# Gated feed-forward with two experts on one Trainium2 core: the rarer expert's weights as a difference to the common one's, formed on GpSimd

## The reference

```
vm = expert_mask(token_type_ids)[..., None]
x = rms_norm(hidden_states, ln_in_w)
mixed = jnp.where(vm, x @ v_qkv, x @ l_qkv)          # q, k, v
...
attn_out = jnp.where(vm, ctx @ v_dense, ctx @ l_dense)
...
mi = rms_norm(hidden_states, ln_post_attn_w)
v_out = jax.nn.silu(mi @ v_gate) * (mi @ v_up) @ v_down
l_out = jax.nn.silu(mi @ l_gate) * (mi @ l_up) @ l_down
hidden_states = hidden_states + jnp.where(vm, v_out, l_out)
```

## Time and profile before

| | us |
|---|---|
| median of 3 runs | 2722.21 |
| lowest, highest | 2719.45, 2730.94 |
| the profiled execution | 2724.13 |
| its span, first to last instruction | 2722.3 |
| mean granted TensorE clock | 0.994 of 2.4 GHz |

### The profile page before, as it was taken

One profiled execution on the slowest core, in us unless ns is written; L12 is line 12 of the kernel. 1 busy time (PEld: TensorE's weight loads), 2 busy tenths in 40 slices (PEclk: granted clock), 3 DMA queues, 4 the chain that ended last, 5 costly groups with the idle time before them and its releaser, 6 DMA issues.

```text
span 2722.3 us, 52680 instructions
## 1 busy us (share of the span) xinstructions
PE 2627.3 (97%) x19429; PEld 1584.6 (58%) x19429; DVE 1624.8 (60%) x3532; ACT 1318.6 (48%) x4818; POOL 974.3 (36%) x862
## 2 busy tenths in 40 slices
PE   6999999999999999999999999999999999999998
PEld 4556566665555656566556565656655556566664
DVE  2426567786424547777643454777855345477874
ACT  2446444654343644464444373555534447255452
POOL 0014344553111515555311241654621133155452
PEclk9999999999999999999999999999999999999999
DMA  7000021212201011120220101112121010120111
GB/s 204 1 24 13 21 55 36 52 29 71 67 1 36 2 31 51 30 64 22 70 63 1 35 2 47 43 30 55 29 71 55 1 36 2 51 58 19 48 29 55
DMA packets 171044, 109.52 MB, mean 40 GB/s; under 512 B 31714, under 2 KB 168356, under 8 KB 170660
## 3 DMA queue, kind: packets, MB, share of 16 engines
q1 hardware_dynamic: 166336, 105.82, 14.0%
q10 hardware_dynamic: 4452, 0.29, 0.1%
HBM read 101.87 MB, written 4.19 MB: 39 GB/s over the span
## 4 chain that ended last, share of the span: by engine, by line
PE 81%; DVE 10%; ACT 5%; issue 2%; POOL 1%; ACTq 1%; DVEq 0%
PE bank L1334 11%; PE bank L1351 6%; PE bank L979 5%; PE bank L1057 5%; PE bank L1239 4%; PE bank L1227 4%; PE bank L1248 4%; PE bank L1220 4%; PE bank L1274 3%; ACT Ebuf L1438 3%; PE bank L1340 3%; PE bank L1033 2%; PE bank L1074 2%; PE bank L1211 2%; PE bank L1017 2%
## 5 line engine op out<-in xcount | busy, mean ns | idle before, releaser
L1839 POOL TENSOR_TENSOR Ebuf<-Ebuf,row_rcp 128x512 f32<-128x512 f32 (+1 forms) x328 | 344.4, 1056 | 956.6 <-DVE row_rcp L1655 956.4
L1438 ACT ACTIVATE Ebuf<-bank,minus_max 128x64 f32<-128x64 f32 x1568 | 468.3, 333 | 116.3 <-DVE minus_max L1639 115.4
L1639 DVE TENSOR_REDUCE minus_max<-bank 128x8 f32<-128x512 f32 (+1 forms) x328 | 220.3, 674 | 226.2 <-PE bank L1017 124.5
L1438 ACT ACTIVATION_READ_ACCUMULATOR Ebuf<-bank,minus_max 128x1 f32 x1568 | 353.5, 225 | 0.0
L1447 ACT ACTIVATE PT<-bank 128x512 f32<-128x512 f32 (+1 forms) x328 | 193.7, 603 | 128.2 <-PE bank L1057 125.8
L1057 PE MATMUL bank<-ident,Ebuf 128*128 128x128 f32 x1296 | 200.9, 281 | 10.0 <-POOL Ebuf L1839 9.5
L1057 PEld LDWEIGHTS bank<-ident,Ebuf 128*128 128x128 f32 x1296 | 146.8, 142 | 79.2 <-issue 46.2
L1334 PE MATMUL bank<-xs_b,w_ring 128*128 128x512 f32 (+1 forms) x384 | 170.0, 605 | 2.4 <-DVE xs_b L1733 2.4
L1334 PE MATMUL bank<-xs_a,w_ring 128*128 128x512 f32 (+1 forms) x384 | 168.8, 602 | 0.0
L966 PE MATMUL bank<-causal_bf,ident_bf 128*128 128x512 bf16 x525 | 136.8, 383 | 0.0
L1881 POOL TENSOR_TENSOR arena_b<-arena_b,masks_b 128x384 f32<-128x384 f32 (+1 forms) x48 | 67.7, 1411 | 192.7 <-DVE arena_b L1809 192.6
(11 more groups left out here) (322 smaller groups left out, 5668.8 us busy)
## 6 DMA issues: line engine op xcount, KB each, us to landing
w_ring<-in_L_W SPq DMA_DIRECT2D x64, 256.0 KB, 3.1
w_ring<-in_L_l_gate SPq DMA_DIRECT2D x80, 128.0 KB, 2.2
w_ring<-in_L_l_up SPq DMA_DIRECT2D x80, 128.0 KB, 2.3
w_ring<-in_L_l_down SPq DMA_DIRECT2D x80, 128.0 KB, 2.2
w_ring<-in_L_v_gate SPq DMA_DIRECT2D x80, 128.0 KB, 2.4
w_ring<-in_L_v_up SPq DMA_DIRECT2D x80, 128.0 KB, 2.4
w_ring<-in_L_v_down SPq DMA_DIRECT2D x80, 128.0 KB, 2.5
arena_a<-in_x SPq DMA_DIRECT2D x4, 512.0 KB
```

The source lines that it names most:

```text
L1438: last = A(Ebuf[:, u % UNITS, cell], bank(token)[:, cell], ACT.Exp, bias=minus_max[:, u % UNITS, c:c + 1], accum_out=row_sum[:, u % UNITS, ...
L1639: V.reduce_max(minus_max[:, u % UNITS, 0:g], cells(bank(token)[:, 0:g * S]), AX_X, negate=True).then_inc(maxed, 1)
L1839: G_.tensor_tensor(v, v, row_rcp[:, n % 3, 0:g].unsqueeze(2).broadcast_to([P, g, S]), ALU.mult).then_inc(probs_ready, 1)
```

## The change

The common expert's products now take every token, unmasked, and the rarer expert's weights are replaced by their difference to the common ones, v - l; x l + (mask x)(v - l) is the same sum. The gate's part is masked, so that the hidden units of the rarer part are silu(g) masked, times u.

- Lines 1726, 1729 and 1814 are gone; `spread` writes xn directly, and lines 1733 and 1853 read xn and write xv. xn_ready is counted once more per half. is_l becomes a constant 1 (`all`) that the attention's line 1757 still reads.
- `u` on VectorE: one product into hid_l, then, after GpSimd's product, one over the late columns: hid_v times u (from PSUM) times 0.5. u's PSUM bank is free after the latter.
- New on GpSimd: `weigh`, three subtractions in the ring for each chunk, after its loads and before TensorE's `g`; a part of `silu`, the late columns of silu_g times is_v into hid_v; once, behind the first `zero_s`, the subtractions of the resident q, k, v and dense weights. The early mask (line 1881) now reads hid_l.
- The plan: new costs (weigh 1.7, silu's GpSimd part 0.45, u on VectorE 1.0 for 2.4, spread 1.75 for 3.45 and 1.15 for 2.0), weigh with its own nominal time, slots given out in the plan's order of weigh and l1h, and both of these held until the slot's last reader has ended and 10 us (`LOADED`) have passed. All engines' lists and the fillers are made anew from this.

```diff
@@ -137,7 +137,7 @@
     for j in range(FT):
-        steps += [(6.4 * j, "g", n, j), (6.4 * j + 1.5, "silu", n, j), (6.4 * j + 2.1, "u", n, j), (6.4 * j + 10.6, "down", n, j)]
+        steps += [(max(0.0, 6.4 * j - 9.0), "weigh", n, j), (6.4 * j, "g", n, j), (6.4 * j + 1.5, "silu", n, j), (6.4 * j + 2.1, "u", n, j), (6.4 * j + 10.6, "down", n, j)]
     return steps + [(6.4 * FT + 6.4, "res3", n)], 6.4 * FT + 6.4
@@ -237,8 +238,10 @@
         return [("POOL", 2.15, None)]
+    if step == "weigh":
+        return [("POOL", 1.7, None)]
     if step == "u":
-        return chain(*(() if where[1] == FT - 1 else (("PE", 2.2),)), ("DVE", 2.4), ("POOL", 1.4))
+        return chain(*(() if where[1] == FT - 1 else (("PE", 2.2),)), ("DVE", 1.0), ("POOL", 1.4))
     if step == "g" and where[1] == FT - 1:
@@ -306,10 +309,12 @@
+    if step == "weigh":
+        return of("PE", ("g", n, last - 1)) if last else of("DVE", ("sums", 5 if n == 2 else 8, 0))
...
-        return of("DVE", ("spread", 5 if n == 2 else 8, 1)) + of(None, ("silu", n, last - 2)) + of("DVE", ("u", n, last - 2))
+        return of(None, ("weigh", *where)) + of("DVE", ("spread", 5 if n == 2 else 8, 1)) + of(None, ("silu", n, last - 2)) + of("DVE", ("u", n, last - 2))
...
-        return of(None, ("silu", *where)) + of("PE", ("down", n, last - 2)) + (of("DVE", ("u", n, last - 1)) if last == FT - 1 else [])
+        return of(None, ("silu", *where)) + of("PE", ("down", n, last - 2)) + of("POOL", ("u", n, last - 2)) + (of("DVE", ("u", n, last - 1)) if last == FT - 1 else [])
@@ -397,10 +403,22 @@
+    def slot():
+        if len(chunks) < SLOTS:
+            return 0.0
+        when = end.get((chunks[len(chunks) - SLOTS][1], "PE"))
+        return None if when is None else when + LOADED
     def room(token):
...
         key = where[0] if where else None
+        if step == "weigh":
+            return slot()
+        if step == "l1h" and where[0] % 2 == 0:
+            there, free = slot(), banks(1)
+            return None if there is None or free is None else max(there, free)
         if step in FILL_STEPS and parts(step, where)[0][0] == "PE":
@@ -796,7 +809,7 @@
-            return {"g": g_ready, "u": h_ready}[step][s].at(turn, FT * li + last + 1)
+            return {"g": g_ready, "u": hv_late}[step][s].at(turn, FT * li + last + 1)
@@ -1317,11 +1330,11 @@
                         rows = P if j < FT - 1 else FR
-                        ring, there = chunk("ffn", s, turn, n, j)
+                        ring, _ = chunk("ffn", s, turn, n, j)
                         w = ffn_weights(ring)[0][step]
...
                         if step == "g":
-                            pe.wait_ge(*there)
+                            pe.wait_ge(*weighed[s].at(turn, FT * (n - 2) + j + 1))
                             if j == 0:
@@ -1345,7 +1358,7 @@
-                        pe.wait_ge(*hl_ready[s].at(turn, FT * (n - 2) + j + 1))
+                        pe.wait_ge(*h_ready[s].at(turn, FT * (n - 2) + j + 1))
@@ -1553,9 +1566,8 @@
                     if j >= 2:
-                        act.wait_ge(*hl_ready[s].at(turn, k - 1))
-                        act.wait_ge(*hv_late[s].at(turn, k - 1))
-                        act.wait_ge(*hv_early[s].at(turn, k - 1))
+                        act.wait_ge(*h_ready[s].at(turn, k - 1))
+                        act.wait_ge(*sv_ready[s].at(turn, k - 1))
                     act.wait_ge(*g_ready[s].at(turn, k + 1))
@@ -1625,7 +1637,7 @@
-                    V.tensor_scalar(st.is_l[:, :], st.is_v[:, :], -1.0, 1.0, ALU.mult, ALU.add).then_inc(masks_ready[s].sem, 1)
+                    V.memset(st.all[:, :], 1.0).then_inc(masks_ready[s].sem, 1)
@@ -1710,8 +1722,8 @@
                     src = st.xn if n in (1, 2) else st.xT
-                    dst, ready = {0: (st.xT, x0_ready), 4: (st.xn, xn_ready), 7: (st.xn, xn_ready), 1: (st.xn, normed),
-                                  2: (st.xn, normed)}.get(n, (st.xv, normed))
+                    dst, ready = {0: (st.xT, x0_ready), 1: (st.xn, normed),
+                                  2: (st.xn, normed)}.get(n, (st.xn, xn_ready))
                     for m in range(DT):
@@ -1720,17 +1732,9 @@
                             V.tensor_scalar(st.xn[:, m, :], st.xn[:, m, :], shift, None, ALU.add).then_inc(xn_ready[s].sem, 1)
-                    if n in (3, 6):
-                        for m in range(DT):
-                            dve.wait_ge(*normed[s].at(turn, STEP_AT[n] + m + 1))
-                            V.tensor_tensor(st.xn[:, m, :], st.xv[:, m, :], st.is_l[:, :], ALU.mult).then_inc(xn_ready[s].sem, 1)
-                    if n in (5, 8):
-                        dve.wait_ge(*normed[s].at(turn, STEP_AT[n] + 2 * h + 2))
-                        V.tensor_tensor(st.xn[:, :, at], st.xv[:, :, at], both(st.is_l[:, at]), ALU.mult).then_inc(xn_ready[s].sem, 1)
                     if n in LATE_AT:
-                        dve.wait_ge(*xn_ready[s].at(turn, XN_AT[n] + (h + 1 if n in HALVED else 2)))
-                        v = late(st.xv[:, :, at])
-                        V.tensor_tensor(v, v, late(both(st.is_v[:, at])), ALU.mult).then_inc(xv_late[s].sem, 1)
+                        dve.wait_ge(*xn_ready[s].at(turn, XN_AT[n] + 2 * h + 2))
+                        V.tensor_tensor(late(st.xv[:, :, at]), late(st.xn[:, :, at]), late(both(st.is_v[:, at])), ALU.mult).then_inc(xv_late[s].sem, 1)
                 if step == "l1v":
@@ -1806,14 +1810,15 @@
                         up = st.g_copy[0:rows, 1 - j % 2, :]
-                    V.scalar_tensor_tensor(out=v, in0=v, scalar=0.5, in1=up,
-                                           op0=ALU.mult, op1=ALU.mult).then_inc(h_ready[s].sem, 1)
-                    dve.wait_ge(*h_ready[s].at(turn, k + 1))
                     if j >= 2:
                         dve.wait_ge(*down_done[s].at(turn, k - 1))
-                    V.tensor_tensor(st.hid_l[0:rows, j % 2, :], v, st.is_l[0:rows, :], ALU.mult).then_inc(hl_ready[s].sem, 1)
-                    V.tensor_tensor(by_batch(st.hid_v[0:rows, j % 2, :])[:, :, LATE:S], by_batch(v)[:, :, LATE:S],
-                                    by_batch(st.is_v[0:rows, :])[:, :, LATE:S], ALU.mult).then_inc(hv_late[s].sem, 1)
+                        dve.wait_ge(*hv_early[s].at(turn, k - 1))
+                    V.scalar_tensor_tensor(out=st.hid_l[0:rows, j % 2, :], in0=v, scalar=0.5, in1=up,
+                                           op0=ALU.mult, op1=ALU.mult).then_inc(h_ready[s].sem, 1)
+                    dve.wait_ge(*sv_ready[s].at(turn, k + 1))
+                    hv = by_batch(st.hid_v[0:rows, j % 2, :])[:, :, LATE:S]
+                    V.scalar_tensor_tensor(out=hv, in0=hv, scalar=0.5, in1=by_batch(up)[:, :, LATE:S],
+                                           op0=ALU.mult, op1=ALU.mult).then_inc(hv_late[s].sem, 1)
                 if step == "res3":
@@ -1844,13 +1849,20 @@
                     G_.memset(st.arena[:, A_VS:A_VS + 2048], 0.0).then_inc(v_zeroed[s].sem, 1)
+                    if turn == 0 and s == 0:
+                        for n in (2, 3):
+                            pool.wait_ge(w_loaded[n], 16 * 9)
+                            for of in (w_qkv, w_dense):
+                                rare, other = of[n, "v"][:, :, :], of[n, "l"][:, :, :]
+                                last = G_.tensor_tensor(rare, rare, other, ALU.subtract)
+                            last.then_inc(w_weighed, 1)
                 if step == "spread" and where[0] in LATE_AT:
...
                     at = span(n, h)
-                    pool.wait_ge(*xn_ready[s].at(turn, XN_AT[n] + (h + 1 if n in HALVED else 2)))
+                    pool.wait_ge(*xn_ready[s].at(turn, XN_AT[n] + 2 * h + 2))
                     for m in range(DT):
-                        v = by_batch(st.xv[:, m, at])[:, :, 0:LATE]
-                        last = G_.tensor_tensor(v, v, by_batch(st.is_v[:, at])[:, :, 0:LATE], ALU.mult)
+                        v, x = (by_batch(some[:, m, at])[:, :, 0:LATE] for some in (st.xv, st.xn))
+                        last = G_.tensor_tensor(v, x, by_batch(st.is_v[:, at])[:, :, 0:LATE], ALU.mult)
                     last.then_inc(xv_early[s].sem, 1)
@@ -1872,13 +1884,31 @@
                         G_.tensor_tensor(*cross_blocks(st, p, r), ALU.mult).then_inc(kbd_built[s].sem, 1)
+                if step == "weigh":
+                    n, j = where
+                    rows = P if j < FT - 1 else FR
+                    ring, there = chunk("ffn", s, turn, n, j)
+                    into, down = ffn_weights(ring)
+                    pool.wait_ge(*there)
+                    for of in "gu":
+                        rare, other = (into[of][e][:, :, 0:rows] for e in "vl")
+                        G_.tensor_tensor(rare, rare, other, ALU.subtract)
+                    G_.tensor_tensor(down["v"][0:rows, :], down["v"][0:rows, :], down["l"][0:rows, :], ALU.subtract).then_inc(weighed[s].sem, 1)
+                if step == "silu":
```

(9 more changed lines are left out.)

43 lines of the change are left out of this document (21 added, 22 removed).

## The result

The changed kernel takes 2742.9 us (median of 20 runs, 2729.0 to 2752.6) against 2720.0 us for the kernel before on the same chips. The ratio of the mean times is 1.0069, 95% interval 1.0054 to 1.0085. It is **slower by 19 us** by the means and by 23 us by the medians, where I forecast 25 us faster. One run of each kernel, at 5210.8 and 7364.7 us, stands far off all others and is in neither the range nor the ratio. The profiled run took 2746.45 us, with a span of 2744.6 and a mean granted clock of 0.990.

The account below looks back on a forecast made before the run. TensorE, busy 97%, was taken as the bound, so only 232 us of its idle time and fillers could give. Direct gain 20, shorter VectorE queue 10, GpSimd loss 5: -25 us, 2697 us against the 2722.2 median; range 2650 to 2750.

Parts of the forecast that it names:

- rival C: Beside attention, weighing on GpSimd delays softmax products and VectorE waits; 30% of 204 us on the path: 2753 us; chance 0.15.
- Steps 1 and 2, 3: VectorE loses 193 us of mask work: 20 us direct gain on the chain, 10 us from its shorter queue.
- Step 4: GpSimd gets 212 us of weighing, late mask and resident subtractions; idle time hides the latter's 8 us at the start.
- Step 5: On GpSimd's fixed queue, 204 us of recurring work delays softmax products: 5 us lost, ends 0 and 102 us.
- Step 6a: TensorE's first matmul on a chunk waits for weighing; at the last chunk 1.3 us fit into 11.5.
- Step 7: GpSimd's new time meets some 850 two-SBUF-input VectorE instructions by chance: 24 us on VectorE, 2 on the path.
- rival D: GpSimd's shared access with VectorE lies on the path: 48 us less the 30 gained, +18, 2740 us; chance 0.07.

Follow-up runs that it names:

- e2: e1 with the streamed weighing left out, GpSimd writing one column per chunk instead; 2690.3 us, ratio 0.9864 to 0.9906.
- e1: Changed kernel with the resident qkv and dense subtractions moved behind stream b's third softmax product; 2733.8 us.
- e9: e1 with the streamed subtractions replaced by three fills of an unread tile, a semaphore between them, and TensorE released first; 2692.7 us.
- e17: e1 with a flag behind each of a chunk's three subtractions instead of one behind the last; 2742.3 us.
- e18: e9 with the three fills replaced by two-input subtractions of resident weights into an unread tile; 2731.7 us.
- e8: Kernel before with the qkv weights' and, of the feed-forward, only the down weights' differences; gate and up weights unchanged; 2702.6 us, ratio 0.9922.
- e19: Kernel before with only the down weights' difference, qkv weights and all norms unchanged; 2708.4 us.
- e14: Kernel before with only the qkv weights' difference, and GpSimd held during each of the 104 reciprocal square roots; 2729.2 us.
- e3: e1 with each chunk's three subtractions replaced by three fills of the ring of about the same length, which read nothing; 2713.9 us.

## Why the prediction was wrong

The direction was wrong, 2742.9 against 2697; that the time lies within the stated 2650 to 2750 is owed to a range that was drawn wide for rival C. In the runs' numbers the change is the sum of -29.9 (all but the weighing, e2 to before), +43.5 (the weighing in the loop, e1 to e2) and +9.1 (the start, changed kernel to e1): +22.7, where I had -30, +5 and 0. By the prediction's steps:

**Steps 1 and 2, 3 (gain on VectorE): right in sum.** The late instruction takes 0.279 us (0.28 foreseen), VectorE is 64% busy beside attention (62 to 65), and the change without its weighing is 29.9 us faster, which is 20 + 10. The split wasn't tested: between the two traces TensorE's idle time is 14.7 us less (95.0 and 80.3), and the fillers that the plan no longer puts in are 16.9 us. VectorE fell by 147 and not 193 us; of the difference the roots' own +34 is the largest piece that I can name.

**Step 4 (GpSimd's time): near by luck, and its cover wrong.** GpSimd has 194 us more, 212 were foreseen. But the weighing alone takes 205.6 us where 167 were foreseen, 0.71 to 0.77 us for a subtraction and not 0.61: the price of 1.78 ns a column was read from the softmax product, and the resident subtractions (3.43 us for 1536 columns, 1.28 for 512) show 2.11. What made up for it is the early mask (line 1881, now 1911), which fell from 129 to 91 us and wasn't in the step. The sentence that failed is that the resident subtractions are hidden by GpSimd's idle time: I took the idle sum of the whole span for the cover of one place. There, a softmax product of stream b was due; price 9 us. e1 puts them where GpSimd is idle.

**Step 5 and rival C (the queue): small, as foreseen.** Waits for softmax products are 7.3 us in e1 against 9.5 before, and 206 us in the queue cost 2.4 us (e9 and e2), where 5 were foreseen. C wasn't it, although the sign came out as C said.

**Step 6a (wait for the weighing): not foreseen, 11.0 us.** I looked at the last chunk alone, where 1.3 us fit into 11.5. At eight other chunks TensorE waited up to 1.8 us. e17 shows that this was not a cost that a finer flag gives back.

**Step 7 and rival D (shared access): the step that decided.** The step had the right rows and 24 us on VectorE, and then took the path's share as VectorE's 10% of the chain: 2 us. Measured: 39 us (e18 against e9), 17 in TensorE's waits for roots, 4 in waits for the keys and 15 in the clock. Three errors are in the step. It counted five two-input steps in a root, where there are seven: of the nine lines only the first two, 1682 and 1685, have one input. That makes 1056 instructions and not 850. It priced them as if each met GpSimd by chance, but the nine steps of a root depend on each other, and where GpSimd runs without a break nearly every two-input step pays a whole instruction: 5.7 us in place of some 1.7 in the worst of them. And a root is not an average piece of VectorE's work: TensorE needs its result for the next norm, and it waited for it before already, 15.6 us in 31 places, which none of the prediction's rows has. D's price of 48 us less 30 gave 2740, near the time that came; its chance of 0.07 was far too low. That its number fits is partly luck: it came from meetings by chance, twice as frequent, and 9 of the 22.7 us are the start, which D didn't have. D's sign on line 1796 (a longer mean) says nothing, by the way: in e2, without weighing, it is 902 and 907 ns, as long as in the changed kernel.

**The clock: not in the sum.** Before and after differ by some 10 us of clock not granted. Among the runs of one and the same changed kernel the four with 0.997 and 0.998 take 2729.0 to 2730.8 us, the one with 0.986 takes 2752.6.

What stays open: why a given order gets the interleaving that it gets; the plan has no entry for the sharing, so its ends (2669.7 for the slowest, 2699.3 for before) don't rank the kernels. Where the weighing is left out, its difference holds: 29.6 us by the plan, 29.9 measured (e2). Open are also why e17's clock is lower, and where the gain of e8 and e19 comes from.

## What to carry to other kernels

Before work goes to GpSimd because it is idle, list the strings of small, dependent two-input instructions on VectorE for which TensorE waits, and price each step of them, at the worst, at one whole GpSimd instruction. A sum of idle time is no cover: ask what is due on the engine at the very place. Take the part of a change that needs the least of the shared resource first; here the down weights' third of the weighing, together with the qkv weights, is faster than the whole, though the qkv part alone is slower than the kernel before: a new order of the engines has to be measured.

## What the runs showed of the hardware that I had not expected

- A VectorE step on 2 columns, 0.16 us alone, takes 0.96 us beside GpSimd's two-input products of 1.0 us and 0.65 beside subtractions of 0.71, each time anew. With GpSimd held, all 104 instances of the third step (1700 of the changed kernel) took 0.160 to 0.164 us (e14).
- GpSimd's fills, which read nothing, left the two-input steps alone. A one-input step between SBUF and SBUF (1697) stood for up to 2.76 us, longer than three fills of 0.715. The Trainium skill, SBUF — State Buffer, "Who interferes with whom", has both: a VectorE instruction with two SBUF inputs contends with a GpSimd instruction that reads SBUF and not with one that only writes, and `tensor_scalar` can enter a mode that takes the ports shared with GpSimd. The trace agrees with the first (the roots' other steps sum in e3 to what they do in e2, e.g. 28.9 us for line 1700); that it was this mode of 1697, no run here shows.
- 39 us lie between two kernels that differ only in whether 288 of GpSimd's instructions read two inputs (763 ns each) or none (716 ns); 21 of them are TensorE's waits for roots and keys, 15 the clock.
